# A two-layer graph network on one core: the first layer's sums are projected once per part of 256 nodes instead of once per pair of groups

## The reference

```python
# layer 0: a relational layer with 8 basis matrices
W = einsum('rb,bio->rio', w_comp, weight)            # 16 relations from 8 bases
msg = einsum('ni,rio->rno', x, W)[etypes, src]
x = layernorm(x + segment_sum(msg, dst) + h_bias)
# layer 1: the mean over the neighbours
deg = maximum(segment_sum(1, dst), 1)
agg = segment_sum(x[src], dst) / deg
x = layernorm(x + x @ W_self + b_self + agg @ W_neigh)
```

## Time and profile before

| | |
|---|---|
| median of 3 runs | 3176.4 us |
| span of the profiled execution | 4143.4 us |
| PE busy | 2142.2 us, 52% |
| DVE busy | 1431.9 us, 35% |
| ACT busy | 332.1 us, 8% |
| POOL busy | 2392.4 us, 58% |
| start of the last wide gather of layer 1 | 2836.0 us |

### The profile page before, as it was taken

How to read it: one execution, slowest core, us unless ns; L and a number is a source line. 1 busy time by engine, 2 the same in 40 slices (tenths; PEclk the granted TensorE clock), 3 DMA queues, 4 the chain that set the end, 5 groups by cost and what they waited for, 6 DMA issues and landing times. The chain is left out here.

```text
span 4143.4 us, 36092 instructions
## 1 busy us (share of the span) xinstructions
PE 2142.2 (52%) x12511; PEld 2001.1 (48%) x12511; DVE 1431.9 (35%) x3693; ACT 332.1 (8%) x668; POOL 2392.4 (58%) x2524
## 2 busy tenths in 40 slices
PE   2455555555655555465555555567144444444445
PEld 1455445555555555455555555566143333333345
DVE  5242222122221222222221221222255657666635
ACT  1110000000000000000000000001000000000001
POOL 6645555555555555555556555565666666666663
PEclk7776666666666666666666665666555666666666
DMA  3832332233332332333333332332112222122222
GB/s 103 240 104 83 93 89 84 83 89 93 87 89 85 93 87 83 87 88 89 87 87 93 88 86 85 87 98 70 47 53 54 54 54 61 53 61 62 61 81 64
DMA packets 257427, 345.24 MB, mean 83 GB/s; under 512 B 47008, under 2 KB 189957, under 8 KB 257238
## 3 DMA queue, kind: packets, MB, share of 16 engines
q0 software_dynamic: 104400, 263.16, 22.7%
q1 hardware_dynamic: 127398, 66.86, 5.5%
q10 hardware_dynamic: 25440, 12.85, 1.0%
HBM read 311.14 MB, written 44.38 MB: 86 GB/s over the span
## 5 line engine op out<-in xcount | busy, mean ns | idle before, releaser
L1639 POOL DMA_INDIRECT rows<-x_x_rows,src_t x1501 | 1427.7, 951 | 1164.2 <-DMA x_x_rows<-xout 463.0
L2241 PE MATMUL zps<-acc,rows 128*128 128x168 f32 x3322 | 761.6, 363 | 570.6 <-issue 461.1
L2241 PEld LDWEIGHTS zps<-acc,rows 128*128 128x128 f32 x3322 | 611.5, 226 | 644.3 <-issue 598.7
L1666 POOL DMA_INDIRECT rows<-x_rows,picked_mem x691 | 655.9, 949 | 347.0 <-issue 196.1
L1887 DVE TENSOR_TENSOR acc<-acc,yps 128x63 f32 (+1 forms) x563 | 123.6, 220 | 1162.2 <-PE yps L2276 966.5
L2255 PEld LDWEIGHTS yps<-oh,rows 128*128 128x128 f32 x2058 | 336.6, 229 | 315.6 <-issue 315.4
L2255 PE MATMUL yps<-oh,rows 128*128 128x21 f32 x2058 | 313.6, 275 | 323.4 <-issue 321.5
L1865 DVE TENSOR_TENSOR acc<-oh,tps 128x1344 f32<-128x1344 f32 x208 | 323.3, 1554 | 141.7 <-remote 108.2
L2376 PE MATMUL zps<-acc,rows 128*128 128x128 f32 x1382 | 274.3, 356 | 121.9 <-issue 117.0
L2376 PEld LDWEIGHTS zps<-acc,rows 128*128 128x128 f32 x1382 | 244.9, 263 | 144.3 <-issue 144.2
L1718 ACT COPY acc<-zps 128x672 f32<-128x672 f32 x208 | 148.2, 714 | 1977.8 <-remote 1786.4
(11 more groups left out here) (315 smaller groups left out, 1882.0 us busy)
## 6 DMA issues: line engine op xcount, KB each, us to landing
rows<-x_x_rows,src_t POOLq DMA_INDIRECT x1501
acc<-in_edge_type_dram SPq DMA_DIRECT2D x207, 64.0 KB
x_x_rows<-zrow ACTq DMA_DIRECT2D x20, 576.0 KB, 3.3
x_x_rows<-in_x_dram SPq DMA_DIRECT2D x20, 576.0 KB
rows<-x_rows,picked_mem POOLq DMA_INDIRECT x691
x_rows<-xout SPq DMA_DIRECT2D x49, 128.0 KB
xin<-in_x_dram SPq DMA_DIRECT2D x48, 128.0 KB
out_dram<-xout SPq DMA_DIRECT2D x24, 256.0 KB
```

Source lines behind the costliest of these rows:

```text
L1639: gather = pool.indirect_dma_start(out=wide_rows[:, g % WIDE_SLOTS, c, :], out_offset=None, in_=table, in_offset=bass.IndirectOffsetOnAxis ...
L1666: pool.indirect_dma_start(out=rows[:, j % SLOTS, c, :], out_offset=None, in_=x1_rows[0:n_nodes, :], in_offset=bass.IndirectOffsetOnAxis(ap ...
L2241: last = nc.tensor.matmul(zwins[g % 2][:, c // HALF, c % HALF // 2], slot_rows(g, c), a[:, g % 4, c], start=(c % 2 == 0), stop=(c % 2 == 1 ...
```

## The change

The projection is done once per *run*: the groups of one part, 4 or 5 of them (`runs`; the first part has two runs, [0,2) and [2,6), and the last part's last group is a run of its own, 51 runs in all). The basis sums of a run are kept in SBUF (`zsb` has 5 places instead of 4), and the 8 matmuls of a run have 336 or 420 columns. Their results go to the bank `tps[1]`, which also takes the transposes and the `loops`. Early sums and degrees stay in pairs in the two banks `ybank`, and are added by `add_pair_windows`, with semaphores of their own; `add_sums` adds the projections alone. A window is so added in two instructions instead of one.

A part is staged after `done_at(k)` groups and turned in the group behind that one, at the same distance for every part; before, it was turned in the group behind the closing pair. `READABLE` goes from 9 to 7 with another rounding. A half may read part k from half 2 x done_at(k) + 7 on; before, from 5 halves behind its closing pair on. For 23 of the 44 parts that are read early this is the same half as before, for 21 it is two halves later; the number of late columns that the formulas of the file give goes from 852 to 856. Stores of the degrees wait for `pair_added`. In the path for edges that aren't sorted the ranges of semaphores are mended; that path is not run with these inputs. Buffers `erep`, `half_i` and `half_v` move.

```diff
-READABLE = 9
+READABLE = 7
+RUN = 5
...
-    def last_pair(k):
-        return (done_at(k) - 1) // 2
-
     def readable(h):
-        return per_group * (max(h - READABLE, 0) // 4 * 2 + 1)
+        return per_group * (max(h - READABLE, 2) // 2 - 1)
 
...
-        sums = first_layer(4 * DUOS * n_bases * SPAN)
-        zsb = sums.rearrange("p (u w b n) -> p u w b n", u=4, w=DUOS, b=n_bases)
+        sums = first_layer(RUN * DUOS * n_bases * SPAN)
+        zsb = sums.rearrange("p (u w b n) -> p u w b n", u=RUN, w=DUOS, b=n_bases)
...
-        half_i, half_v = (sb(name, [P, etiles + 2 * groups], I32) for name in ("half_i", "half_v"))
+        half_i = rdeg[:, 0, WIN:WIN + etiles + 2 * groups].bitcast(I32)
+        half_v = rdeg[:, 1, 0:etiles + 2 * groups].bitcast(I32)
...
+            runs = []
+            for k in range(all_parts):
+                g0, g1 = done_at(k - 1) if k else 0, done_at(k)
+                middle = [2] if k == 0 else [last_group] if k == last_part else []
+                bounds = [g0] + middle + [g1]
+                runs += [(r0, r1, k, r0 == g0) for r0, r1 in zip(bounds[:-1], bounds[1:])]
+            run_of = {g: r for r, (r0, r1, k, first) in enumerate(runs) for g in range(r0, r1)}
...
+            staged_at = {done_at(k): k for k in range(all_parts)}
+            turned_at = {done_at(k) + 1: k for k in range(all_parts)}
             out_at = dict(turned_at)
...
-            loops_at = {(1, 3, 7, 11)[k]: k for k in range(len(quads))}
+            loops_at = {(2, 3, 4, 8)[k]: k for k in range(len(quads))}
...
+            ybank1 = tps[1][:, :, :].rearrange("p t e -> p (t e)")
+            windows = [y[:, 0:2 * 2 * DUOS * SPAN].rearrange("p (k w n) -> p k w n", k=2, w=2 * DUOS) for y in ybank]
+
+            def sums_col(g):
+                r0, r1, k, first = runs[run_of[g]]
+                return (g - (done_at(k - 1) if k else 0)) * DUOS * SPAN
...
-                            sp.wait_ge(w1.group_added, groups)
+                            sp.wait_ge(pair_added, groups)
...
+                            sp.wait_ge(pair_added, done_at(k))
...
-                            after(act, w1.y_done, g // 2 - 1)
-                            nc.scalar.copy(zsb[:, g % 4].rearrange("p (h w) b n -> p h (w b n)", h=2),
+                            after(act, w1.y_done, run_of[g])
+                            nc.scalar.copy(zsb[:, kept_at(g)].rearrange("p (h w) b n -> p h (w b n)", h=2),
                                            zduos[g % 2]).then_inc(w1.z_copied, 1)
...
-                    def add_sums(g):
-
-                        first = 1 if narrow(g) else 0
+                    def starts_of(g):
                         _, starts = nc.values_load_multi_w_load_instructions(
                             base[0:1, g * DUOS:g * DUOS + duos_of(g)], engines=DVE_ONLY, min_val=0, max_val=n_nodes,
                             skip_runtime_bounds_check_because="clamped to the number of nodes, and acc is padded")
-                        dve.wait_ge(w1.y_done, products_before(g))
+                        return starts
+
+                    def add_pair_windows(g):
+
+                        first = 1 if narrow(g) else 0
+                        starts = starts_of(g)
+                        dve.wait_ge(deg_done, g // 2 + 1)
+                        after(dve, pair_added, g)
+                        for c in range(duos_of(g)):
+                            target = kinds3[:, 2 * first:3:2, bass.ds(starts[c], SPAN)]
+                            if c:
+                                dve.wait_ge(pair_step, g * (DUOS - 1) + c)
+                            add = nc.vector.tensor_tensor(target, target, windows_of(g)[:, first:2, c, :], ALU.add)
+                            add.then_inc(pair_step if c < duos_of(g) - 1 else pair_added, 1)
+
+                    def add_sums(g):
+
+                        starts = starts_of(g)
+                        dve.wait_ge(w1.y_done, run_of[g] + 1)
                         after(dve, w1.group_added, g)
                         for c in range(duos_of(g)):
-                            target = kinds3[:, first:3, bass.ds(starts[c], SPAN)]
+                            target = mem[:, bass.ds(starts[c] + SHIFT, SPAN)]
+                            y0 = sums_col(g) + c * SPAN
                             if c:
                                 dve.wait_ge(w1.rmw, g * (DUOS - 1) + c)
-                            add = nc.vector.tensor_tensor(target, target, windows_of(g)[:, first:3, c, :],
-                                                          ALU.add)
+                            add = nc.vector.tensor_tensor(target, target, ybank1[:, y0:y0 + SPAN], ALU.add)
...
-                        if g % 2 == 0 and 2 <= g < groups:
-                            add_sums(g - 2)
-                            add_sums(g - 1)
-                        if groups <= g < groups + 2:
-                            add_sums(g - 2)
+                        if g % 2 == 0 and 2 <= g <= groups:
+                            add_pair_windows(g - 2)
+                            add_pair_windows(g - 1)
+                        if g in run_ends:
+                            for e in range(*runs[run_ends[g]][0:2]):
+                                add_sums(e)
...
-                                bank_free("pair", g // 2)
-                            if g == last_group:
-                                bank_free("single", g)
+                                after(pe, pair_added, g - 2)
...
-                    def project_pair(p):
-                        pe.wait_ge(w1.z_copied, 2 * p + 2)
-                        two = zsb[:, 2 * p % 4:2 * p % 4 + 2].rearrange("p u w b n -> p (u w) b n")
...
+                    def project(r):
+
+                        r0, r1, k, first = runs[r]
+                        pe.wait_ge(w1.z_copied, r1)
+                        if first:
+                            after(pe, n1.added, k)
+                        else:
+                            pe.wait_ge(w1.group_added, r0)
+                        if r == 1:
+                            pe.wait_ge(s_loopc, len(quads) - 1)
+                        if r == 2:
+                            pe.wait_ge(s_loopc, len(quads))
+                        duos = (r1 - r0) * DUOS if r1 < groups else (last_group - r0) * DUOS + duos_of(last_group)
+                        kept = zsb[:, 0:r1 - r0].rearrange("p u w b n -> p (u w) b n")
+                        y0 = sums_col(r0)
...
-                            project_pair(g // 2)
+                        if g + 1 in run_ends:
+                            project(run_ends[g + 1])
```

117 lines of the change are left out of this document (41 added, 76 removed).

## The result

The changed kernel takes 3183.8 us (median of 14 runs, 3182.7 to 3191.6); the kernel before, in 14 runs beside them, 3176.2 (3175.0 to 3180.6). The ratio is 1.0028, with a 95% interval of 1.0020 to 1.0036: slower by 7.6 us where 6 were forecast. Ten of the fourteen runs lie between 3182.7 and 3184.6 and four between 3189.4 and 3191.6; the profiled one is of the four.

What follows compares the result with a forecast made beforehand. POOL's gathers, 1.22 to 1.25 us each, were taken to bound the kernel. Terms +5.0 (gathers), 0, 0, 0 and +1 (joint) made +6 on 3176.4, forecast 3182 us; own range 3172 to 3194, wider range 3125 to 3265.

Steps and rivals of the forecast that it cites:

- What bounds the kernel: POOL: 2512 gathers at 1.22 to 1.25 us each set the time; the runs have next to no waits.
- Gathers, +5.0: POOL's row: 856 late columns for 852, four gathers more at 1.25 us, +5.0 us, nothing hides them.
- Projection, 0: PE: 105 projections become 51, columns equal in sum, so work per part hardly changes and stays hidden; cost 0, saving 0.
- Additions, +128 busy and hidden: DVE: 831 additions become 831 smaller ones and 831 more; +128 us busy, hidden behind POOL's gathers as throughput.
- The chain of a part, a wait of 0: From a part's last gather to its store: 22.0 to 35.9 us against 34.2 until the first reader; full clock taken, 0.
- a PE that is never idle has the full clock: PE's clock in the projection step: 3.00 busy of 3.00 at 1.00, so the lower clock would not be the bound.
- the stored part comes too late: POOL's wait before a part's first reader: at the lower clock 1.7 us for each of 44 parts, 3257 us; chance 0.26.
- The joint, +1: Layer 1's end: last pair's early sums and degrees precede the last projection's additions on DVE; up to 3.3 us, 1 taken.
- that rival: POOL's waits for stored parts: runs have them, longer lookahead relieves 21 parts by 3 us each, 3119 us; chance 0.20.
- DVE against POOL: POOL's descriptors: every added DVE instruction stops POOL for its own length, +146 us, 3328 us in all; chance 0.02.

Runs made afterwards that it cites:

- kernel before (unchanged): Nothing changed against the kernel before, run again for a second profile; 3176.7 us.
- The split alone: Kernel before with early sums and degrees added in one instruction and the projection in another; 3194.0 us, ratio 1.0038; on a slower chip 4347.8 us, 1.0358.
- the edit that would test it: Changed kernel with DVE scaling the next group ahead of a run's additions; 4304.3 us, ratio 1.0262; with `READABLE` 6 also, 1.0649 and 1.0665.
- last pair's additions moved: Changed kernel with the additions of the last pair's windows put behind those of the last part's sums; 3194.5 us, ratio 1.0042.

## Why the prediction was right, and which steps of it weren't

**What bounds the kernel: right in the main, wrong about the cause.** POOL with its gathers at 1.25 us bounds it, and the runs have next to no waits: in the kernel before they have none. The pace of 1.22 as the lower end isn't found; it is 1.25, and the cover with it 35.0 us instead of 34.2. But the 997 us of the first profile are not a matter of "the profiled execution" against the runs: on two of four chips every run is like that, and the forecast was right for the other sort alone. On the first sort the change is small because the chain is mostly covered, on the second it is large because the chain is on the path, as the earlier trace rows showed. (A slip in the reading of the earlier trace rows: the form of 168 columns is eight times as large as that of 21, not twice.)

**Gathers, +5.0: right**, by the price of 1.23 us that 13 added columns showed: 4.9 for four.

**Projection, 0: right as throughput, wrong as work.** The projections fell from 452.3 us (1680 records) to 340.8 (816), so that fewer records did save time. But the basis sums, which nothing changed, went up:

```profile
L2257 PE MATMUL zps<-acc,rows 128*128 128x168 f32 x3322 | 833.0, 415 | 206.5 <-DMA rows<-x_x_rows,src_t 188.4 <-DVE acc L1870 7.7 <-ACT acc L1723 5.3
```

In the kernel before (unchanged) they are

```profile
L2241 PE MATMUL zps<-acc,rows 128*128 128x168 f32 x3322 | 718.1, 372 | 360.3 <-DMA rows<-x_x_rows,src_t 333.5 <-DVE acc L1865 12.6 <-ACT acc L1718 8.5
```

The mean granted clock is 0.649 instead of 0.682. The basis sums take 115 us more, the early sums 69, the coefficients (L2244) 31, and the projections 112 less; with smaller groups that makes the 109 us more on PE. As throughput it costs nothing, since PE still waits 188 us for the rows. In the chain of a part it counts, because a group and a half of this work stands ahead of the transposes.

**Additions, +128 busy and hidden: the size right, the cover wrong in kind.** 124.7 us were measured. DVE has the room as throughput, but a run's 16 to 20 additions stand in its queue as one piece of 6 to 8 us, and what is behind it is awaited: the scaling by PE, the statistics by the next store. The split alone, in the kernel before with its shorter cover, costs 0.38%.

**The chain of a part, a wait of 0: the value taken was wrong, and that it hardly shows is luck.** Before, 18.0 us was 2 to 4 too few. After, 22.0 to 35.9 was worked out, and the full clock chosen for a PE "behind 10 us of unbroken projection", with 11 us to spare. The longest chain of the changed kernel is 36.5 us, a little above the upper end, and there is nothing to spare. PE does reach the full clock inside the projection (1.00 from 1527), but the sum has no term for what comes next: DVE's queue keeps the scaling behind the additions, PE is idle for up to 6.0 us, and its group and a half runs at 0.50. Nor does "a PE that is never idle has the full clock" hold: from 2054 to 2078 it is never idle and has 0.50. That no more than 2.5 us of waits came of it in the profile is owed to the cover of 35.0 us: with four gathers less the same working would have forecast no wait again (22.0 against 29.3), and 34 us net were measured. The rival "the stored part comes too late" named the place and the clock rightly, but it is a few parts that are late and not 44. That the scaling's place is what lowers the clock on this sort of chip is read from the timeline; the edit that would test it ran on the other sort only.

**The joint, +1: about the right size for what it names, but the wait is another's.** POOL waits 5.2 us net there in the profiled run. The kernel before (unchanged) at the joint, from its last wide gather over ACT's copies of the last two groups' sums to the last store of x1:

```profile
2089.88 0.95 POOL L1639 DMA_INDIRECT rows<-x_x_rows,src_t  x1 [0.30 <-issue]
...
2091.84 0.70 ACT L1718 COPY acc<-zps 128x672 f32<-128x672 f32 x1
...
2100.16 0.72 ACT L1718 COPY acc<-zps 128x672 f32<-128x672 f32 x1 [7.62 <-PE zps L2241]
...
2108.53 0.40 SPq L1529 DMA_DIRECT2D x_rows<-xout  x1
```

and the changed kernel:

```profile
2092.33 0.95 POOL L1644 DMA_INDIRECT rows<-x_x_rows,src_t  x1 [0.30 <-issue]
...
2099.19 0.69 ACT L1723 COPY acc<-zps 128x672 f32<-128x672 f32 x1
...
2106.53 0.72 ACT L1723 COPY acc<-zps 128x672 f32<-128x672 f32 x1 [6.65 <-PE zps L2257]
...
2116.19 0.40 SPq L1533 DMA_DIRECT2D x_rows<-xout  x1
```

| us | last wide gather to first copy | to second copy | to the store |
|---|---|---|---|
| kernel before (unchanged) | 1.96 | 8.32 | 8.37 |
| changed kernel | 6.86 | 7.34 | 9.66 |
| last pair's additions moved | 1.66 | 7.70 | 9.96 |

The additions of the last pair lie in the last step, with 1.3 us more than before; +1 was forecast. (This step varies by as much: with `READABLE` 13 the kernel before takes 9.86 there, its last projection running at the lower clock.) The other 3.9 of the 5.2 us come from the first two steps, 4.9 more and 1.0 less, and the 4.9 from PE, which had fallen behind its rows at the lower clock (0.50 until 2078). The third row has the same instructions up to the second copy, and no such lag. So this term too hangs on the clock of PE behind the scaling, for which the sum has no term; what brings the clock back sooner in one run than in the other isn't shown.

**The other rivals.** On the first sort of chip there was no wait to be relieved. On the second there was, and a longer lookahead pays as that rival said (0.951 with `READABLE` 9); the seven halves of the change are too few there. DVE against POOL: the trace gives it nothing again, 949 ns per gather before and 950 after with 125 us more on DVE.

The sum came out near because its one large term, +5.0, holds, and because what it left out happened to stay small: +1 stands for some 2.6 us of waits in the median (7.7 in the profiled run), at the joint and behind the chain.

## What to carry to other kernels

Whether an engine can take more work in the sum says nothing on whether others wait for what stands behind that work: look in its queue for the next instruction that another engine awaits, and count the added piece against that one's slack, together with the work that the other engine does at the lower clock after it has waited. How much slack a lookahead has is measured most cheaply by making it shorter a step at a time until the first waits come. When an experiment removes a wait, compare also the stretch ahead of the edited instructions: if that has moved too, the edit may not be the cause. And before a profile is weighed against the runs, see whether its own time agrees with theirs: where it doesn't, both ways of running may be real, and a change can cost 0.3% in one and 4.6% in the other.

## What the runs showed of the hardware

The two sorts of chips were not expected: 3176 and 3183 us on two, 4155 and 4204 on two others for one kernel. A wide gather takes 947 to 952 ns on all of them, and one starts every 1.25 us while nothing holds POOL. What the rows of the slower ones show is that many long waits for a semaphore end when POOL has stopped issuing gathers. The changed kernel on a slower chip:

```profile
1501.74 0.96 PE L2269 MATMUL yps<-oh,rows 128*128 128x21 f32 x8
...
1532.69 0.72 ACT L1723 COPY acc<-zps 128x672 f32<-128x672 f32 x1 [37.52 <-remote]
1533.02 0.95 POOL L1644 DMA_INDIRECT rows<-x_x_rows,src_t  x1 [5.10 <-remote]
...
1533.47 6.55 PE L2297 MATMUL tps<-acc,picked_mem 128*128 128x336 f32 x16 [30.76 <-ACT acc L1723]
```

PE's last work on the group is over at 1502.7; ACT, which copies the group's sums, begins at 1532.7, some 5 us after POOL has run out of slots and stopped. PE is idle for 30.76 us in between. It isn't so everywhere: of the 99 waits of ACT and DVE in layer 1 of this profile that are longer than 5 us and whose releaser is "remote", 73 end in a stop of POOL of more than 1 us, and 26 while it goes on issuing. Why a chip does this was not found out.
